# A cross-attention loop on one core: score products split by bank behind ring jobs, and the value products' places changed

## What is computed

```python
# cross-attention; Q = layernorm(x), K = V = context
Qh = _split_heads(Q @ Wq.T + bq)
Kh = _split_heads(K @ Wk.T + bk)
Vh = _split_heads(V @ Wv.T + bv)
scores = einsum('bhqd,bhkd->bhqk', Qh, Kh) / sqrt(8)
scores = scores - jnp.max(scores, axis=-1, keepdims=True)
attn = softmax(clip(scores, -1e9, 1e9), axis=-1)
attn = clip(attn, 1e-12, None)
attn = attn / sum(attn, axis=-1, keepdims=True)
x = x + (einsum('bhqk,bhkd->bhqd', attn, Vh) merged) @ Wo.T + bo
...
x = x + self_attention(layernorm(x))    # 16 heads, 128 keys
x = x + experts(layernorm(x))           # up 128->512, gelu, down 512->128, top 4 of 16
```

## Time and profile before

| | |
|---|---|
| median of three runs | 210.49 us |
| the profiled execution | 210.37 us, of which the span of the engines is 208.4 us |
| PE busy | 190.9 us (92% of the span) |
| DVE, ACT, POOL busy | 145.7, 143.6, 81.5 us |
| score products of the first tile, t = 0 | start at 39.39 us |
| score products of t = 8, 16, 24, 32 | 49.81, 59.62, 69.42, 79.78 us |
| first expert product | 130.66 us |

### The profile page before, as it was taken

The page is one execution under the profiler, slowest core; times in us unless marked ns, Lnnn a source line. Parts: engine busy times, 40 slices in busy tenths (PEclk is TensorE's granted clock), DMA queues, the critical chain, the costliest instruction groups (busy, mean ns, idle before and its releaser), DMA issues.

```text
span 208.4 us, 6357 instructions
## 1 busy us (share of the span) xinstructions
PE 190.9 (92%) x2558; PEld 132.3 (63%) x2559; DVE 145.7 (70%) x263; ACT 143.6 (69%) x321; POOL 81.5 (39%) x113
## 2 busy tenths in 40 slices
PE   4889899799999989999999999999879999999991
PEld 1335437255555545554554666897858998999981
DVE  5296488999999988999999944756984438222220
ACT  4768684488989897786796977686674545446660
POOL 6223679989899991110201001420000005078400
PEclk9999999999999999999999999999999999999999
DMA  5835332336437422327887750500000000000000
GB/s 119 285 151 216 118 98 89 93 94 228 159 101 198 122 81 82 97 67 234 277 296 211 213 190 6 203 2 0 3 0 3 0 0 13 3 0 5 0 0 20
DMA packets 8688, 21.24 MB, mean 102 GB/s; under 512 B 1664, under 2 KB 2784, under 8 KB 8656
## 3 DMA queue, kind: packets, MB, share of 16 engines
q1 hardware_dynamic: 7344, 19.47, 29.1%
q0 software_dynamic: 592, 0.74, 1.6%
q10 hardware_dynamic: 720, 0.59, 0.9%
HBM read 17.52 MB, written 3.28 MB: 100 GB/s over the span
## 4 chain that ended last, share of the span: by engine, by line
PE 73%; DVE 13%; ACT 4%; DMA 3%; issue 2%; POOL 2%; ACTq 1%; DVEq 0%
PE ps L1267 15%; PE ps L1516 13%; PE ps L1549 10%; PE ps L1248 10%; PE ps L1208 6%; PE ps L1113 4%; DVE mx L600 4%; DMA wks<-in_wk 3%; PE ps L1120 2%; PE ps L1407 2%; PE ps L1132 2%; POOL wr L496 1%; DVE sm L711 1%; PE ps L1413 1%; DVE kst L709 1%
## 5 line engine op out<-in xcount | busy, mean ns | idle before, releaser
L1025 ACT ACTIVATE ex<-ps 128x512 f32<-128x512 f32 x128 | 69.5, 595 | 15.7 <-PE ps L1248 12.8
L600 DVE TENSOR_REDUCE mx<-ps 128x2 f32<-128x1024 f32 x64 | 74.9, 1218 | 7.7 <-PE ps L1208 7.7
L1267 PE MATMUL ps<-ex,vau 128*9 128x128 f32 x1024 | 40.0, 274 | 0.5 <-ACT oS L1037 0.4
L1516 PE MATMUL ps<-xT,w1s 128*128 128x128 f32 x256 | 34.4, 278 | 0.2
L1516 PEld LDWEIGHTS ps<-xT,w1s 128*128 128x128 f32 x256 | 31.1, 192 | 1.6 <-ACT cT L1048 0.8
L1267 PEld LDWEIGHTS ps<-ex,vau 128*9 128x9 f32 x1024 | 22.1, 90 | 15.7 <-ACT ex L1025 11.8
L806 DVE SCALAR_TENSOR_TENSOR xs<-ps,wr,xs 128x128 f32<-128x128 f32 x32 | 11.2, 350 | 28.6 <-PE ps L1549 28.3
L1048 ACT ACTIVATE cT<-ps,b1s 128x128 f32<-128x128 f32 x64 | 18.2, 370 | 13.8 <-PE ps L1516 13.8
L1048 ACT ACTIVATE ex<-ps,b1s 128x128 f32<-128x128 f32 x64 | 18.1, 369 | 13.0 <-PE ps L1516 12.9
L1208 PE MATMUL ps<-kst,qst 64*128 64x512 bf16 x128 | 25.0, 381 | 1.9 <-DVE mx L600 1.8
L1248 PE MATMUL ps<-qst,kst 64*128 64x128 bf16 x512 | 25.5, 217 | 0.5 <-ACT ex L1025 0.4
(11 more groups left out here) (211 smaller groups left out, 255.3 us busy)
## 6 DMA issues: line engine op xcount, KB each, us to landing
kst<-parts_d SPq DMA_DIRECT2D x84, 64.0 KB
w1s<-in_w SPq DMA_DIRECT2D x8, 512.0 KB, 4.1
kst<-in_w SPq DMA_DIRECT2D x8, 512.0 KB, 4.8
parts_d<-w1s SPq DMA_DIRECT2D x4, 768.0 KB, 3.8
cT<-in_ctxT SPq DMA_DIRECT2D x3, 512.0 KB, 5.7
cT<-in_ctxT SPq DMA_DIRECT2D x2, 256.0 KB, 4.8
picks<-in_pick ACTq DMA_DIRECT2D x1, 384.0 KB, 5.3
qkvs<-in_qkvw POOLq DMA_DIRECT2D x1, 192.0 KB, 3.6
```

What stands on the lines that cost most here:

```text
L600: dve.tensor_reduce(out=mx2[:, b, 2 * pair:2 * pair + 2, f], in_=ps[:, bank:bank + 2, :], axis=AX.X, op=ALU.max).then_inc(s["redA"], 1)
L1025: act.activation(ex[:, e % NE, :], ps[:, EBANK["exp", e], :], ACT.Exp, scale=SCALE).then_inc(s["exp"], 1)
L1267: last = pe.matmul(ps[32 * j:32 * j + DK + 1, 7, 128 * hg:128 * hg + 128], vau[:, NK * b + c, GH * hg + j, :], ex[:, (2 * t + j % 2) % NE, ...
L1516: last = pe.matmul(ps[:, SELF[j % 2], 128 * n:128 * n + 128], w1s[:, f0:f0 + 128], xT[:, (b % B) * S:(b % B + 1) * S], start=True, stop=True)
```

## The change: what it does

Three things are done.

First, behind each ring job the score products of a tile are split. If tile t-1 had a ring job, PE issues the four products of half 0, then the unit, then the four of half 1; each half waits for its own bank only.

Second, three of the value pieces of the second batch (5, 6 and 7) leave the opening and become ring jobs of the loop, behind the scores of tiles 3, 11 and 19 (`VALS_AT`). Pieces 2, 3 and 4 move later in the opening. The first units move earlier: unit 0 now stands behind the third pick of key rows, units 1 to 3 between the other picks. The filler matmuls (`fill`, seven in all, a product that nothing reads) are gone. ACT's copies follow the new order. The first tile waits for five pieces.

Third, POOL's and SP's lists follow: `max_terms(0)` goes from DVE to POOL, between `k_parts(4)` and `k_parts(5)`; `max_terms(1)` to `(4)` shift among the squares and the DMA issues; and the two writes of the second batch's terms (`parts_out(2)`, `(3)`) now stand behind the stacks of pairs 5 and 6 in place of behind pair 7.

The diff, cut to its core:

```diff
         SMALL_AT = {34: "sums", 36: "heads", 39: "proj", 41: "normed", 43: "qkv", 47: "qkT"}
+        VALS_AT = {3: 5, 11: 6, 19: 7}
         SELF_EXP_AT = {53: [0], 54: [1], 55: [2], 57: [3]}
...
+        def turns(t):
+            return t % 8 == 6 and t + 2 < TILES
+        def ring_job(t):
+            return turns(t) or t in SMALL_AT or t in VALS_AT
         def weight_jobs():
...
                 out += [("exp", 2 * t), ("exp", 2 * t + 1)]
-                if t % 8 == 6 and t + 2 < TILES:
+                if turns(t):
                     out.append(("turn", t // 8 + 1))
...
                     out.append((SMALL_AT[t], 0))
+                if t in VALS_AT:
+                    out.append(("vals", VALS_AT[t]))
             return out
...
-        V_BANK = [2, 3, 2, 3, 5, 6, 4, 5]
+        V_BANK = [2, 3, 5, 7, 5]
         K_BANK = [0, 1, 0, 1, 4, 5, 6, 4]
...
                 stack(0, p)
-            parts_out(2)
-            parts_out(3)
+                if p >= PAIRS - 3 and p < PAIRS - 1:
+                    parts_out(p - PAIRS + 5)
             for n in range(2, 2 * B):
...
                 k_parts(n)
+                if n == NG:
+                    max_terms(0)
+            max_terms(1)
             tmp = alibi[:, 0:4, :].rearrange("p h k -> p (h k)")
...
                 pool.wait_ge(s["ksq"], c + 1)
-                if c == 0:
-                    max_terms(1)
-                if c == 2:
+                if c == 1:
                     max_terms(2)
+            max_terms(3)
             for dst, src in ((wos[:], wo), (boB[:], bo.broadcast_to([128, D])), (qkvs[:], qkvw), (projs[:], projw),
...
                 pool.dma_start(dst, src).then_inc(d_const, 16)
-                if src is tri_in:
-                    max_terms(3)
...
             ones(6, 8)
+            max_terms(4)
             pool.wait_ge(d_const, 16 * N_CONST)
...
                                     sl8[:].unsqueeze(2).broadcast_to([128, H, 128]), ALU.mult))
-            max_terms(4)
             link(pool.memset(neg[:], -1.0))
...
                     dve.tensor_reduce(out=mx[:, b, hs], in_=mx2[:, b, hs, :], axis=AX.X, op=ALU.max).then_inc(s["mxd"], 1)
-                if u == 7:
-                    dve.wait_ge(s["mxd"], 1)
-                    dve.wait_ge(s["init"], 1)
-                    m = mpad[:, 0].rearrange("p r (a c) -> p (r a) c", a=2)
-                    link(dve.tensor_copy(m[:, :, 0], mx[:, b, hs]))
-                    link(dve.tensor_tensor(mxr[:], mx[:, b, hs], m[:, :, 0], ALU.subtract))
-                    link(dve.tensor_copy(m[:, :, 1], mxr[:]))
-                    dve.tensor_tensor(m[:, :, 2], mxr[:], m[:, :, 1], ALU.subtract).then_inc(s["mpad"], 1)
...
             k_set(2)
-            v_piece(2, V_BANK[2])
+            q_set(1)
             k_set(3)
-            v_piece(3, V_BANK[3])
-            q_set(1)
             q_set(2)
...
                 k_plain(NG + n)
-            for n in range(NG, 2 * NG):
-                v_piece(n, V_BANK[n])
+            v_piece(2, V_BANK[2])
+            v_piece(3, V_BANK[3])
             def clip_exps(b):
...
             rows(0)
+            v_piece(4, V_BANK[4])
             for t in range(TILES):
...
                 exps(t, 1)
-                if t % 8 == 6 and t + 2 < TILES:
+                if t in VALS_AT:
+                    v_piece(VALS_AT[t], EBANK["vals", VALS_AT[t]])
+                if turns(t):
                     rows(t // 8 + 1)
...
-            def vals(n):
-                bank = V_BANK[n]
+            def vals(n, bank):
                 for j in range(4):
...
                         pe.wait_ge(s["mrow"], i + 1)
+                    elif kind == "vals":
+                        pe.wait_ge(s["va"], i + 1)
                     elif kind == "sums":
...
                 if u == 1:
-                    pe.wait_ge(s["va"], 4)
+                    pe.wait_ge(s["va"], 2)
                 if b == 0 and f == 0 and pair in (0, 2, 4):
...
-            def fill(n):
-                pe.wait_ge(s["init"], 1)
-                for _ in range(n):
-                    pe.matmul(ps[:, 7, :], fq[:, 0, 0, :], kst[:, 0, ON_CHIP, 0:512], start=True, stop=True)
             def turn(g):
...
                     pe.wait_ge(s["init"], 2)
-                    pe.wait_ge(s["va"], NG + 2)
+                    pe.wait_ge(s["ksq1"], 3)
                 bank_free(("turn", g))
...
-            def scores(t):
+            def scores(t, halves=(0, 1)):
...
                 b, r0 = g // NG, 2 * (g % NG)
-                if c0 == 0:
+                if c0 == 0 and 0 in halves:
                     pe.wait_ge(s["mrow"], g + 1)
-                if t == 0:
-                    pe.wait_ge(s["va"], 2 * NG)
-                bank_free(("exp", 2 * t))
-                bank_free(("exp", 2 * t + 1))
-                last = [None, None]
+                if t == 0 and 0 in halves:
+                    pe.wait_ge(s["ksq1"], NG)
+                    pe.wait_ge(s["va"], 5)
+                for a in halves:
+                    bank_free(("exp", 2 * t + a))
+                last = {}
                 for c in range(2):
                     for r in range(2):
-                        for a in range(2):
+                        for a in halves:
                             half = slice(HALF * a, HALF * a + HALF)
...
                                                 tile_position=(HALF * a, 0))
-                last[0].then_inc(s["scB"], 1)
-                last[1].then_inc(s["scB"], 1)
+                for a in halves:
+                    last[a].then_inc(s["scB"], 1)
...
             pe.wait_ge(d_wv, 16)
-            vals(0)
+            vals(0, V_BANK[0])
             key_rows(1)
-            vals(1)
+            vals(1, V_BANK[1])
             key_rows(2)
-            pe.wait_ge(s["va"], 1)
-            vals(2)
+            unit(0)
+            query_rows(1)
+            unit(1)
             key_rows(3)
-            pe.wait_ge(s["va"], 2)
-            vals(3)
-            query_rows(1)
-            unit(0)
+            unit(2)
             query_rows(2)
-            unit(1)
-            pe.wait_ge(s["kset"], NG)
+            unit(3)
             keys(4)
-            unit(2)
+            unit(4)
             keys(5)
-            unit(3)
+            unit(5)
+            unit(6)
             pe.wait_ge(s["qset"], len(Q_ROUNDS))
             keys(6)
-            unit(4)
+            unit(7)
             pe.wait_ge(s["ksq1"], 1)
             keys(7)
-            unit(5)
+            unit(8)
             pe.wait_ge(s["ksq1"], 2)
-            vals(4)
-            unit(6)
-            pe.wait_ge(s["ksq1"], 3)
-            vals(5)
-            unit(7)
-            pe.wait_ge(s["ksq1"], 4)
-            vals(6)
-            unit(8)
-            pe.wait_ge(s["va"], NG + 1)
-            vals(7)
+            vals(2, V_BANK[2])
             unit(9)
-            fill(3)
+            vals(3, V_BANK[3])
+            unit(10)
             turn(0)
-            fill(3)
-            unit(10)
-            fill(1)
+            pe.wait_ge(s["va"], 3)
+            vals(4, V_BANK[4])
             unit(11)
...
+            def next_unit(t):
+                if t + 8 + LEAD < N_UNITS:
+                    unit(t + 8 + LEAD)
             for t in range(TILES):
-                scores(t)
-                if t % 8 == 6 and t + 2 < TILES:
+                if ring_job(t - 1):
+                    scores(t, (0,))
+                    next_unit(t)
+                    scores(t, (1,))
+                else:
+                    scores(t)
+                if turns(t):
                     turn(t // 8 + 1)
...
                     small(SMALL_AT[t])
-                if t + 8 + LEAD < N_UNITS:
-                    unit(t + 8 + LEAD)
+                if t in VALS_AT:
+                    bank_free(("vals", VALS_AT[t]))
+                    vals(VALS_AT[t], EBANK["vals", VALS_AT[t]])
+                if not ring_job(t - 1):
+                    next_unit(t)
                 self_first(t)
...
                     values(t - 1)
...
```

## The result

The changed kernel takes 209.56 us (median of five runs, 209.22 to 209.81) beside 210.65 for the kernel before: a ratio of 0.9947 [0.9929, 0.9966]. In a second session it was 209.35 beside 210.50, 0.9938 [0.9915, 0.9962]. So it is faster by some 1.1 us; the forecast, 210.4, was no measurable change. Some executions of these kernels take 1.5 to 2% longer as a whole, and the ratios here leave them out. The profiled execution took 209.72, its span is 207.8 (208.4 before).

What follows compares the result with a forecast made beforehand. PE carries 73% of the waits; in the loop the ring of exps and score products sets 1.17 us a tile. Terms -5.04 - 0.57 + 4.35 + 0.60 + 0.2 + 0.4 = -0.06 gave 210.4 us, range 208.9 to 211.8.

Steps and rivals of the forecast that it cites:

- the likeliest case: Whole kernel: the forecast itself, 210.4 us, own range 209.8 to 211.0; chance 0.44.
- Term 1: Opening: first tile's score products start at 34.35 instead of 39.39, 5.04 us less; 3.27 of it is three moved pieces.
- Term 2: First two tiles: DVE is no longer behind, so they take 2 x 1.17 instead of 2.91; 0.57 us less.
- Terms 3 and 4: Loop: three value pieces cost 1.45 each, 4.35 us more; splits behind four turns cost 0.15 each, 0.60 more.
- cheap halves: Split tiles: a half alone takes 0.11, so the total is 1.6 us less, 208.8; in part, 209.6; chance 0.24.
- the ring: Loop: exp 0.60, wait 0.15, next exp 0.42 later set a tile's 1.17 us; PE has 0.06 to spare.
- Term 5: Turn 4: PE waits 0.6 to 0.8 for POOL's maxima, no less than before; 0.2 us more (0 to 0.6).
- Term 6: From tile 35 on: nine more splits, partly hidden in waits between DVE and PE; 0.4 us more (0 to 1.35).
- the rival of 0.15 each: Tiles 35 to 55: all nine splits cost 0.15 each, 0.95 more than taken, 211.4 us; chance 0.22.
- cheap halves, in part: Split tiles: the partial form of the rival that a half alone takes 0.11; 209.6 us; cheap halves' chance 0.24.

## Where the prediction held and where it missed

The measured 209.56 is within the whole range of 208.9 to 211.8, but outside the 209.8 to 211.0 of the likeliest case.

**Term 1, the opening (-5.04): right to 0.36, and to 0.1 in the second session.** The place of each unit came out, the 0.5 of waiting for unit 8's transfers was 0.79 and 0.57. That these rows are the bound up to there shows in the trace with every tile split: its clock was at 0.50 from 13.3 to 16.8, unit 0 came 0.8 later (19.99), and unit 8 still started at 29.37, without a wait. The split between its parts held too: 3.27 forecast for the three pieces, 3.25 measured. What I had not seen is that the units among the picks also take over the work of the fillers: in the changed opening the idle times are 0.46, 0.79, 0.46 and 0.54, spread from 22 to 36 us, and its clock never falls, while the old opening without fillers lost about 1.3 us to the clock. "The rest is filler and waits" counted the fillers as time on the path; they were free.

**Term 2 (-0.57): right**, -0.59 from tile 0 to tile 2.

**Terms 3 and 4 (+4.35 and +0.45 up to tile 30): the step that failed.** Measured +3.70. It said that a half alone lasts as long as both, 0.21, and then put three streams of 0.21 one behind the other, so that a split tile is 1.31 or 1.32. A split tile is 1.17: the second four start 0.30 after the first, the sign I had named for cheap halves. Not because four products take 0.11: they take 0.23 (40.55 to 40.78), about what I gave them. What failed is that the streams follow each other. The two halves of the rows need not start in the order written, and work of the other half fills the gap. Products and unit take 0.61 in the split tile (40.55 to 41.16), not the 0.74 of the sum, and 0.55 in a plain one (41.72 to 42.27): 0.06 more. Up to tile 30 the ring leaves PE that 0.06 in every tile, so a split costs nothing there; from tile 32 on it cost 0.03 to 0.06. The length of rows 2 and 6 speaks only of all eight together. A second, smaller error: the piece was given a turn's start, 0.49 behind its tile's products, and starts 0.39 behind them (38.19 to 38.58). A piece with a split behind it then costs 1.21 in tiles 3 to 5 (4.70 in place of 3.49), not 1.45, and a turn's split next to nothing. The other half of that step was right: the split gains nothing behind a turn, since PE's order holds the products back.

**Term 5 (+0.2): right in kind**, +0.36 with the split; the idle time is 0.99, not 0.6 to 0.8. The reason that I gave (all issues behind group 3's maxima) is what moving the issues and moving the units both showed. I missed that the unit which those maxima wait for stands behind piece 7.

**Term 6 (+0.4): measured +0.23**, and the rival of 0.15 each is out: undoing the splits gives 0.27 back, and 12 more cost 0.06 each.

**Not in the sum: +0.39 behind the loop**, 0.35 of it at one DVE instruction whose code and neighbours did not change. The three traces of the old program (the second profile of before and the one without fillers are two of them) don't have it, and all eleven of the changed one and of the kernels made from it do. The same two instructions start without it in the second batch, 32 us later.

Cheaper splits and pieces are 1.1 less than the forecast, turn 4 level with it, tile 32 on 0.17 less, the opening 0.33 more, the end 0.39 more: together 0.54 under the -0.06 of the sum. The likeliest case fell, and the rival "cheap halves, in part" came out at the 209.6 it gave. That it did so to the tenth is luck: cheaper splits and pieces were worth 1.27, nearer to the 1.6 of that rival in full, and a later opening and the stretch behind the loop, neither of them in it, took 0.7 back. The other 0.3 between the medians is the profiled executions' own: 210.37 was 0.12 below the median shown of before, 209.72 is 0.16 above that of the changed kernel.

## What to carry to other kernels

Before pricing a reordering, ask of each step in a loop what it waits for, and write first what waits for nothing: here that was worth 1.3 us, as much as the whole change, most of it by way of another engine's list, at a turn eleven tiles on. A wait that a row does not note is found by adding the lengths from start to start. The fillers here, in time that PE waited for DVE anyway, cost nothing and held the clock: before such matmuls are taken out, see that real work closes the gaps.

## What the runs showed of the hardware

- Matmuls on different row halves (tile positions 0 and 64) start out of program order: a unit's matmul at 40.62 ahead of products at 40.67 written before it. Eight products of 64 rows by 128 columns take 0.23 both alternating and in two blocks of four (70.46 to 70.69). The Trainium skill, TensorE: Matmul & The Clock Gate, Part 3, The mechanism, has matmuls start and end strictly in program order; for different row halves this trace does not agree.
- Without the fillers the granted clock fell to 0.50 (1.2 GHz) from about 42 on, after idle times of 0.73, 0.73, 0.74 and 0.61 between 36.1 and 40.3, and was back at 1.00 (2.4 GHz) by 46; idle times of 0.46, 0.79, 0.46 and 0.54 between 22.2 and 35.9 in the changed opening left it at 1.00.
- Two stops stand where the code is the same: 0.89 on PE in the middle of 16 like matmuls (without the fillers), and 0.35 more between two DVE instructions (changed kernel). Transfers of instructions stand beside both. For PE they are told above. For DVE, an 8 KB packet of that kind starts 0.7 to 1.0 after the stop in each of the eleven traces that have it (147.49 in the changed kernel, for 146.82); in the three that don't, it starts at 140.13, 140.36 and 142.23, 7.3 us ahead of the second instruction. This fits a place in the instruction stream that a change further up has shifted, but no run was made that tests it.
